# The chain of row roots in two pieces inside unit 3, its statistics written and spread at later points of SP's order

## What is computed

```python
def attn(h):                                   # h: layer-normed x
    q, k, v = heads(h @ Wq + bq), heads(h @ Wk + bk), heads(h @ Wv + bv)
    ctx = local_attention(q, k, v)             # blocks of 128 queries, windows of 256 keys
    idx = [0] + top_62_by_norm(q) + [t - 1]    # per batch and head
    ctx[idx] = softmax(q[idx] @ k.T / 8) @ v   # global rows replace the local ones
    return ctx
x = x + attn(layernorm(x))
x = x + layernorm(x) @ (W * scale[:, None]).T + b
```

## Time and profile before

| | |
|---|---|
| runs | 2225.85, 2229.26, 2229.56 us |
| profiled execution | 2226.99 us, span of the core 2225.40 us, mean granted TensorE clock 0.99 |
| TensorE matmul | 2153.6 us busy (97%) |
| VectorE | 1485.7 us (67%) |
| ScalarE | 828.9 us (37%) |
| GpSimd | 598.5 us (27%) |
| chain that ended last | TensorE 87%, VectorE 7%, issue 3%, ScalarE 2% |

### The profile page before, as it was taken

One profiled execution on the slowest core, in us unless ns is written; L12 is line 12 of the kernel. 1 busy time (PEld: TensorE's weight loads), 2 busy tenths in 40 slices (PEclk: granted clock), 3 DMA queues, 4 the chain that ended last, 5 costly groups with the idle time before them and its releaser, 6 DMA issues.

```text
span 2225.4 us, 38393 instructions
## 1 busy us (share of the span) xinstructions
PE 2153.6 (97%) x12768; PEld 1835.7 (82%) x12768; DVE 1485.7 (67%) x2989; ACT 828.9 (37%) x2186; POOL 598.5 (27%) x464
## 2 busy tenths in 40 slices
PE   5999999999999999999999999999999979999999
PEld 4888888878888888788888887888888867888887
DVE  6587667664877676648776766486656566666664
ACT  2334435452354455523444555235444440000000
POOL 1332223124321231243213312432132113211221
PEclk9999999999999999999999999999999979999999
DMA  3332131104321211143122110321121112333331
GB/s 142 95 98 72 59 68 62 52 29 122 96 65 67 61 67 52 32 122 96 62 70 65 64 53 29 102 78 48 47 78 42 33 67 111 141 132 135 129 141 66
DMA packets 116723, 175.35 MB, mean 79 GB/s; under 512 B 16208, under 2 KB 81814, under 8 KB 116624
## 3 DMA queue, kind: packets, MB, share of 16 engines
q1 hardware_dynamic: 108688, 155.25, 21.6%
q10 hardware_dynamic: 4608, 16.78, 1.9%
q0 software_dynamic: 3328, 2.17, 0.4%
HBM read 122.73 MB, written 51.44 MB: 78 GB/s over the span
## 4 chain that ended last, share of the span: by engine, by line
PE 87%; DVE 7%; issue 3%; ACT 2%; POOL 0%; DMA 0%; DVEq 0%; SPq 0%; POOLq 0%; ACTq 0%
PE proj L519 42%; PE proj L791 15%; PE pv L642 9%; PE turn L632 5%; PE score L617 5%; PE pv L686 3%; PE score L667 2%; PE misc L654 1%; PE turn L782 1%; PE turn L677 1%; ACT xT_hi L832 1%; PE turn L560 1%; DVE xT_lo L1143 1%; ACT probs L904 1%; DVE ln_stats L1064 1%
## 5 line engine op out<-in xcount | busy, mean ns | idle before, releaser
L519 PE MATMUL proj<-xT_hi,w_hi 128*128 128x512 f32 x1536 | 401.3, 403 | 6.6 <-DVE xT_lo L1143 5.3
L519 PE MATMUL proj<-xT_hi,w_lo 128*128 128x512 f32 x1536 | 407.5, 397 | 0.0
L519 PE MATMUL proj<-xT_lo,w_hi 128*128 128x512 f32 x1536 | 381.2, 390 | 0.0
L519 PEld LDWEIGHTS proj<-xT_lo,w_hi 128*128 128x128 f32 x1536 | 288.3, 188 | 62.4
L519 PEld LDWEIGHTS proj<-xT_hi,w_lo 128*128 128x128 f32 x1536 | 280.9, 188 | 62.5 <-issue 0.2
L519 PEld LDWEIGHTS proj<-xT_hi,w_hi 128*128 128x128 f32 x1536 | 275.7, 189 | 61.7 <-issue 6.0
L904 ACT ACTIVATE probs<-score,neg_max 128x256 f32<-128x256 f32 (+1 forms) x512 | 229.1, 460 | 172.5 <-DVE neg_max L1231 97.4
L412 POOL TENSOR_TENSOR ctx_out<-pv_sum,row_inv 128x256 f32<-128x256 f32 x128 | 84.3, 659 | 678.4 <-DVE pv_sum L1268 646.8
L388 POOL CAST w_hi<-w_raw 128x1024 fp32r<-128x1024 f32 x96 | 113.8, 1186 | 521.5 <-PE proj L519 365.1
L390 POOL TENSOR_TENSOR w_lo<-w_raw,w_hi 128x1024 fp32r<-128x1024 f32 x96 | 231.5, 2412 | 7.8
L642 PE MATMUL pv<-v_nat,pT_lo 128*128 128x128 f32 x1024 | 198.9, 276 | 0.0
(11 more groups left out here) (147 smaller groups left out, 3458.9 us busy)
## 6 DMA issues: line engine op xcount, KB each, us to landing
w_raw<-in_wstream SPq DMA_DIRECT2D x96, 512.0 KB, 4.4
x_buf<-in_rows SPq DMA_DIRECT2D x56, 512.0 KB, 3.3
q_rows<-q_nat SPq DMA_DIRECT2D x64, 256.0 KB, 2.9
ctx_rows<-ctx_out SPq DMA_DIRECT2D x128, 128.0 KB, 1.8
q_store<-ctx_rows SPq DMA_DIRECT2D x32, 512.0 KB, 4.1
out<-q_store ACTq DMA_DIRECT2D x32, 512.0 KB, 2.6
q_store<-in_cols SPq DMA_DIRECT2D x28, 512.0 KB, 4.1
q_store<-in_rows SPq DMA_DIRECT2D x8, 512.0 KB, 5.0
```

Of the source, the lines that this page charges most:

```text
L519: mm = pe.matmul(proj[:, bank, :], w[b][:, k * P:k * P + P], x[:, k, half * HALF:half * HALF + HALF], start=(m == 0), stop=(m == 23), skip ...
```

## The change

`roots` gets stages: stage 0 makes the aggregates, the variance and the first guess (five links with the opening one), stage 1 the three Newton steps. `row_roots(n, stage)` is called at place 3 (stage 0) and place 4 (stage 1) of unit 3, no longer at the end of unit 2. `save_stats` moves from behind unit 2 to between the third and the fourth store of unit 3. `spread_stats` (`spread_scale` in the last batch) moves from behind unit 3 to unit 4, behind the column and the first weight slice and ahead of the first store.

```diff
+GUESS_LINKS = 5
+LN_LINKS = GUESS_LINKS + 3 * NEWTON
...
-            def stores(n, hp, next_slices):
+            def stores(n, hp, next_slices, following):
                 if next_slices:
                     sp.wait_ge(w_split[0], n * BUFS + PAIRS // 2 + 3 + hp)
                     sp.dma_start(w_raw[0][:, :], next_slices[0]).then_inc(raw_in[0], 16)
+                if hp == HALF_PAIRS:
+                    if following:
+                        spread_stats(n)
+                    else:
+                        spread_scale(n)
                 store_ctx(n, hp, 0)
                 store_ctx(n, hp, 1)
...
                 store_ctx(n, hp, 2)
+                if hp == HALF_PAIRS - 1 and following:
+                    save_stats(n)
                 store_ctx(n, hp, 3)
...
                     if hp == 2:
                         load_last_column(n, following)
-                        if following:
-                            save_stats(n)
-                    if hp == 3:
-                        if following:
-                            spread_stats(n)
-                        else:
-                            spread_scale(n)
...
-            def row_roots(n):
-
-                dve.wait_ge(rows_seen, n * TILES + TILES)
-                apart(dve)
-                dve.sem_inc(ln_step, 1)
-                roots(FIRST_STEPS + n * LN_LINKS, TILES)
-                dve.sem_inc(stat_set, 1)
+            def row_roots(n, stage):
+
+                if stage == 0:
+                    dve.wait_ge(rows_seen, n * TILES + TILES)
+                    apart(dve)
+                    dve.sem_inc(ln_step, 1)
+                roots(FIRST_STEPS + n * LN_LINKS, TILES, stages=(stage,))
+                if stage == 1:
+                    dve.sem_inc(stat_set, 1)
...
                 top_norms(3)
+                if following and hp == HALF_PAIRS - 1:
+                    row_roots(n, 0)
                 columns(3)
                 pv_sums(u, 2)
                 gq_lo_out(u)
                 p_lo_out(u, 3)
                 inverses(u, 3)
                 top_norms(4)
+                if following and hp == HALF_PAIRS - 1:
+                    row_roots(n, 1)
                 columns(4)
                 global_maxima(u)
...
                 if following and hp < HALF_PAIRS - 1:
                     row_moments(n, hp + 1)
-                if following and hp == HALF_PAIRS - 2:
-                    row_roots(n)
                 columns(6)
```

More of the change, by code:

```diff
@@ L42 @@
 ROOT_GUESS = 0x5F3759DF
-LN_LINKS = 5 + 3 * NEWTON
+GUESS_LINKS = 5
+LN_LINKS = GUESS_LINKS + 3 * NEWTON
 SKIP = float(1 << 20)
@@ L318, in batch @@
                     if hp < PAIRS - 2:
-                        stores(n, hp, [wstream[PAIRS + 4 + 2 * hp], wstream[PAIRS + 5 + 2 * hp]])
+                        stores(n, hp, [wstream[PAIRS + 4 + 2 * hp], wstream[PAIRS + 5 + 2 * hp]], following)
                     else:
                         i = 2 * (hp - PAIRS + 2)
-                        stores(n, hp, [wstream[i], wstream[i + 1]] if following else None)
+                        stores(n, hp, [wstream[i], wstream[i + 1]] if following else None, following)
                     if hp < 2 and following:
@@ L1068, in moments, with roots @@
                     stats.then_inc(ln_step, 1)
-            def roots(steps, size=1, at=0, between=None):
-                links = [1]
+            def roots(steps, size=1, at=0, between=None, stages=(0, 1)):
+                links = [1 if 0 in stages else GUESS_LINKS]
                 link = link_of(steps, links, between)
@@ L1075, in roots @@
                                                                                       ln_sq, ln_less))
-                dve.wait_ge(ln_step, steps + 1)
-                apart(dve)
[L1078 to L1090, removed]
+                if 0 in stages:
+                    dve.wait_ge(ln_step, steps + 1)
+                    apart(dve)
+                    for i in range(at, at + size):
+                        last = dve.bn_aggr(ln_mv[:, i, :], ln_stats[:, i, :, :].rearrange("p a b -> p (a b)"))
+                    link(last)
+                    dve.tensor_scalar(minus_half, ln_mv[:, at:at + size, 1], EPS, -0.5, ALU.add, ALU.mult)
+                    link(dve.tensor_scalar(var, ln_mv[:, at:at + size, 1], EPS, None, ALU.add))
+                    link(dve.tensor_scalar(bits, var.bitcast(U32), 1, None, ALU.logical_shift_right))
+                    link(dve.tensor_scalar(rstd.bitcast(U32), bits, -1.0, float(ROOT_GUESS), ALU.mult, ALU.add))
+                    assert links[0] == GUESS_LINKS
+                if 1 in stages:
+                    for _ in range(NEWTON):
+                        link(dve.tensor_tensor(sq, rstd, rstd, ALU.mult))
+                        link(dve.tensor_tensor(less, sq, minus_half, ALU.mult))
+                        link(dve.scalar_tensor_tensor(rstd, less, 1.5, rstd, ALU.add, ALU.mult))
+                    assert links[0] == LN_LINKS
             def normalise(src, dst, i, done):
```

## The result

The changed kernel takes **2212.89 us** in the median of four runs (2211.96 to 2214.84), against 2227.56 for the kernel before in the same rounds (2225.84 to 2229.56): ratio 0.9935, 95% interval 0.9924 to 0.9947. In a second set with five runs it took 2212.86 against 2227.75, ratio 0.9936 (0.9922 to 0.9949). The profiled execution took 2213.43 us, its span is 2211.8, 13.6 under the span of before. Forecast were 2214.5 and, from the own time of the profiled execution, 2213.3.

The account below looks back on a forecast made before the run. TensorE was taken as the bound, idle at unit 3's start for VectorE's chain. Terms: -13.7 and four zeros, giving 2213.3 from the profiled execution, 2215.6 from the median; forecast the middle, 2214.5, range 2210.5 to 2219.5 us.

Parts of the forecast that it names:

- -13.70 us: Start of unit 3, first three batches: TensorE's gaps behind VectorE's chain (10.04 us) and the slow running behind them go.
- The 3.66 us for the slow clock: TensorE behind the three gaps: time run slow after each, 1.77, 1.69 and 0.20 us, expected to go too.
- The two pieces: VectorE, places 3 and 4 of unit 3: 1.84 and 1.81 plus 0.1 us, hidden in idle 3.02 and 2.66; price 0.
- The upper bound of 14.2 us: SP's queue: longest time from the first statistics write's issue until the statistics are written, before the spread.
- 3 to 5 were called likely: Unit 4: us by which the spread lands before VectorE reads it, 0.5 in the worst case; price 0.
- Rival (b): Start of unit 4: small writes slow the queue, the spread comes late and VectorE waits; 2229.8 to 2264 us, chance 0.06.
- Rival (a): Unit 3: a piece overruns its idle stretch or the clock's part doesn't come back; 2217 to 2220 us, chance 0.10.

Follow-up runs that it names:

- Run 2: The changed kernel with the chain's first piece (aggregates to first guess) back at the boundary behind unit 2, the second left in unit 3: 2218.75 us, ratio 0.9961.
- run 9: The kernel before, with GpSimd's subtraction for the low part of the key weights cut to 128 of 1024 columns: 2213.56 us against 2228.62, ratio 0.9945.
- Runs 8 and 10: The kernel before, statistics written in 32-byte DRAM runs; the second also writes roots for both statistics, making the source contiguous: 2227.57 and 2226.50 us.
- run 3: The changed kernel with both chain pieces at place 3 of unit 3, one behind the other: 2213.51 us, ratio 0.9931.
- run 4: The changed kernel with the spread issued right behind the writing of the statistics, ahead of unit 3's fourth store: 2213.81 us, ratio 0.9933.
- Run 5: The changed kernel's VectorE pieces in unit 3, but SP writes and spreads the statistics at its old places: 2237.24 us against 2226.99, ratio 1.0048.
- run 7: The changed kernel with five unused reductions over 1024 elements behind the second piece, at place 4 of unit 3, first three batches: 2226.79 us, ratio 0.9997.
- run 12: The changed kernel with GpSimd's key split of unit 7 later and unit 6's value split held until three low parts are done: 2200.70 us, ratio 0.9879.

## Why the prediction was right

**The bound and its price.** The gap was VectorE's lateness at the start of unit 3, and the distance of the marks was its whole price. Predicted -13.70 us, found 13.67 in the intervals, 13.6 in the span, 14.7 and 14.9 between the medians. Run 2 shows the dose: part of the chain back, part of the gap back. The 3.66 us for the slow clock were right to take in: without them the sum would have been 2217, outside what was measured. But their size was read from one execution. Behind the third of its gaps, of 3.35 us like the second, the granted clock stayed at 1.00, so its 0.20 us is no slow clock; gaps behind which the clock stayed up cost 0.2 us beyond themselves in runs 2 and 9 too. Runs 8 and 10 leave VectorE's order as before: by their marks the same three gaps cost 14.81 and 13.52 us, with the clock down behind three and two of them. So the third digit of the agreement is luck, and the price is 13.5 to 14.8.

**The two pieces.** Price 0, as predicted. The term itself was mis-sized: piece one measured 1.40, not 1.84 us, since the 0.44 us of waiting ahead of the aggregates at the old place are absent at the new one, where they begin right behind the multiplication of q (305.19). So 1.64 us stayed idle where 1.2 were forecast. Piece two measured 1.75 where it was 1.91, which leaves 1.00 before the mark and not 0.7. The split wasn't needed: run 3 has the same time with both pieces at place 3. The wait for GpSimd went, as the rows of GpSimd said, and run 9 shows that it was that wait and not the operation's place behind the aggregates. The rule of the Trainium skill ("SBUF — State Buffer", "Who interferes with whom") is borne out by the trace: 1.34 us with GpSimd at work, 0.17 without.

**The writing and the spread.** The upper bound of 14.2 us was safe; the writes landed after 8.5 and 10.5. The spread took 7.0 us, not the 4.8 of before, with a column and a slice ahead of it (5.0 in run 4 with nothing ahead), so it lands about 2 us ahead of its use where 3 to 5 were called likely. Rival (b) named the small writes as the cause of a slow queue, and runs 8 and 10 bear that out. But it needed the queue to stay slow whatever the writes' age, and that isn't so: the column issued at 323.29, just behind the landing of the second write, took 4.5 us. Run 5, where store, column and weights stand right behind the writes and SP's wait, shows that late transfers can cost 22 us.

**The time.** From the own time of the profiled execution the sum was 2213.3, and it was measured as 2212.9. The middle with the median of the three runs shown, 2214.5, was 1.6 too high, because that median (2229.26) was high for this kernel: with more runs it was 2226.4 to 2228.6.

**Rival (a)** is void: neither piece overruns, and the clock came back in full.

## What to carry to other kernels

Price a gap of the bounding engine by the distance of two marks around it, not by the idle time alone: what runs slow behind it may belong to it. Do so in more than one execution, since the clock fell behind seven of nine such gaps, and check that nothing else ends later: at the end of a batch the slow clock made the interval only 0.1 us longer. A chain of small operations costs nothing where its engine already waits for another one; the steps of the DMA queue that depend on it must move with it, or the queue's wait takes the gain and more. Look beside a stretched instruction of VectorE for what GpSimd does at that time: here moving GpSimd's work by a few microseconds was worth almost as much as the change.

## What the runs showed of the hardware

- TensorE's clock fell behind some gaps and not behind others of the same length. Gaps of 1.41 us (run 2) and 2.18 us (run 9), three each, left it at its upper level. Behind those of 3.34 and 3.35 us in the three traces with VectorE's order as before (the kernel before, runs 8 and 10) it fell to its lower level, a granted clock of 0.50, in seven of nine cases, and behind the three of 3.0 us in run 7 in all. Where it fell the time lost behind the gap was 1.5 to 1.8 us, else 0.2. The gaps of 4.97, 5.13 and 4.30 us of run 5 lost 3.1, 1.7 and 2.8.
- Shorter gaps were followed by a fall too. The pair of 0.96 and 1.78 us at the end of a batch stands 33 times in eleven of the traces, and the clock fell behind the second gap in 11 of them. The gap of 1.92 us in the last batch had the clock down within 3 us in 5 of 14 traces.
- Writes to DRAM in runs of 4 bytes land late: in the changed kernel the packets of both show as done by 314.6, and the writes landed at 320.7 and 323.2. They hold the transfers behind them: 12.9 us for 512 KB behind 2107 small packets, 8.9 behind 1232, 3.7 behind 336. The Trainium skill ("DMA: Bandwidth & Descriptors", "Specifications") has transfers under 512 B as read-modify-write; that this is the reason was not tried here.
- VectorE's operations with two inputs in memory were held by GpSimd's as well, not only the small tensor_scalar: three low parts took 5.36 us with GpSimd at work and 1.89 without (run 12).
